# The low-rank product of a four-layer residual chain: x_hi against both halves of the adapters in one matmul, and the gates' part of h2 with the adapters as weights

## Time and profile before

| what | value |
|---|---|
| median of three runs | 701.98 us |
| the profiled execution | 701.46 us |
| its span | 699.6 us |
| granted clock of TensorE, mean | 1.0 |
| busy VectorE, ScalarE, GpSimd | 49%, 40%, 13% |
| phase 2 of group 0 | from 250.23 us |

### The profile page before, as it was taken

One profiled execution on the slowest core, in us unless ns is written; L12 is line 12 of the kernel. 1 busy time (PEld: TensorE's weight loads), 2 busy tenths in 40 slices (PEclk: granted clock), 3 DMA queues, 4 the chain that ended last, 5 costly groups with the idle time before them and its releaser, 6 DMA issues.

```text
span 699.6 us, 9550 instructions
## 1 busy us (share of the span) xinstructions
PE 674.9 (96%) x3432; PEld 581.4 (83%) x3432; DVE 345.9 (49%) x529; ACT 276.7 (40%) x415; POOL 87.6 (13%) x128
## 2 busy tenths in 40 slices
PE   4899999999999999999999999999999999999997
PEld 4789989899999988788789878789878878887886
DVE  4779999999822355025633022741321652302352
ACT  4637484955422442115640022652121553012353
POOL 2300115003010021001210000211000121000020
PEclk9999999999999999999999999999999999999999
DMA  9921312001000115002881001694000586000272
GB/s 258 330 79 30 91 31 61 1 4 57 1 0 1 61 48 217 0 1 95 292 297 60 0 0 40 227 308 167 0 0 0 168 276 230 11 1 0 91 231 100
DMA packets 39315, 67.61 MB, mean 97 GB/s; under 512 B 3572, under 2 KB 23028, under 8 KB 39284
## 3 DMA queue, kind: packets, MB, share of 16 engines
q1 hardware_dynamic: 34672, 58.81, 26.3%
q10 hardware_dynamic: 4612, 8.39, 3.3%
HBM read 58.80 MB, written 8.39 MB: 96 GB/s over the span
## 4 chain that ended last, share of the span: by engine, by line
PE 75%; DVE 10%; ACT 6%; DMA 4%; SPq 2%; issue 2%; POOL 1%; ACTq 0%; DVEq 0%
PE ps L916 25%; PE ps L917 24%; PE ps L918 24%; DVE tmp L737 3%; ACT tmp L502 2%; DMA raw<-w_t 2%; DVE ring_lo L667 2%; DMA e_lo_w<-w_t 2%; DVE w_w L746 1%; DVE tmp L740 1%; DVE w_w L727 1%; DVE w_w L733 1%; DVE tmp L743 1%; ACT raw L480 1%; PE ps L1059 1%
## 5 line engine op out<-in xcount | busy, mean ns | idle before, releaser
L916 PE MATMUL ps<-e_hi,ring_hi 128*128 128x384 f32 (+3 forms) x384 | 134.2, 349 | 11.5 <-DVE e_lo L667 10.1
L667 DVE TENSOR_TENSOR ring_lo<-raw,ring_hi 128x512 fp32r<-128x512 f32 x128 | 89.5, 718 | 91.2 <-ACT ring_hi L594 91.0
L918 PE MATMUL ps<-e_hi,ring_lo 128*128 128x384 f32 (+3 forms) x384 | 133.9, 349 | 0.0
L594 ACT ACTIVATE ring_hi<-raw 128x512 fp32r<-128x512 f32 x128 | 78.2, 628 | 76.7 <-PE ps L918 49.7
L916 PE MATMUL ps<-x_both,e_hi 128*128 128x512 f32 x256 | 102.2, 399 | 2.5 <-DVE e_mid L897 2.5
L916 PE MATMUL ps<-ring_hi,e_mid 128*128 128x512 f32 x256 | 100.0, 391 | 3.6 <-DVE ring_lo L667 3.6
L917 PE MATMUL ps<-x_both,e_hi 128*128 128x512 f32 x256 | 101.2, 395 | 0.0
L918 PE MATMUL ps<-x_both,e_lo 128*128 128x512 f32 x256 | 100.7, 393 | 0.0
L917 PE MATMUL ps<-ring_lo,e_mid 128*128 128x512 f32 x256 | 99.7, 389 | 0.0
L918 PE MATMUL ps<-ring_hi,e_mid 128*128 128x512 f32 x256 | 99.6, 389 | 0.0
L916 PEld LDWEIGHTS ps<-e_hi,ring_hi 128*128 128x128 f32 x384 | 72.7, 189 | 17.3 <-DVE e_lo L667 10.1
(11 more groups left out here) (140 smaller groups left out, 902.6 us busy)
## 6 DMA issues: line engine op xcount, KB each, us to landing
raw<-w_t SPq DMA_DIRECT2D x64, 512.0 KB, 4.8
w_w<-w SPq DMA_DIRECT2D x16, 512.0 KB, 5.0
xraw<-x_t SPq DMA_DIRECT2D x16, 512.0 KB, 4.5
y<-tmp ACTq DMA_DIRECT2D x32, 256.0 KB, 3.2
e_lo_w<-w_t SPq DMA_DIRECT2D x4, 512.0 KB, 10.1
e_lo_w<-w_t SPq DMA_DIRECT2D x4, 384.0 KB, 5.8
e_mid_w<-bs SPq DMA_DIRECT2D x24, 64.0 KB, 2.7
e_mid_w<-b_cat SPq DMA_DIRECT2D x1, 512.0 KB, 7.6
```

The source lines that it names most:

```text
L594: act.activation(ring_hi[:, (2 * k + h) % 4, :], raw[:, k % RAW, h * 512:(h + 1) * 512], ACT.Copy).then_inc(w3_hi, 1)
L667: return dve.tensor_tensor(out, whole, hi.bitcast(F32), ALU.subtract)
L916: pe.matmul(out, a[0], b_[0], start=start, stop=False, **kw)
L918: return pe.matmul(out, a[1], b_[0], start=False, stop=stop, **kw)
```

## The change

Three things change together.

1. `low_rank`. The two halves of E now lie in one tensor, and one matmul with x_hi as weights has both halves moving. The tile is 152 columns (128 + 8 + the 16 of its own sequence only), so this matmul has 2 x 152 = 304 columns, in two runs of SBUF, and the one with x_lo has 152. Each token tile has a bank of its own, 4 to 7, with the two parts side by side. ScalarE copies the right part to SBUF (`tok`) and VectorE adds the left one; only then do the logits start. `low_rank` waits for `y_free` at 8g + 8 instead of 8g + 4.
2. The order in the tile: sequence 0's adapter columns stand behind the logits, sequence 1's ahead of the experts. GpSimd's `now` makes one copy over both halves where it made two; in group 0 the second sequence's columns are in place already.
3. h2. `turn_h2` moves ahead of `turn_g`, takes the adapter columns out of `tok` and writes bank 5. `h2_add` then has br_now as weights (32 columns, zero in the other sequence's place) and the gated tiles moving, 256 columns at a time, 6 matmuls, added in bank 5. The factor 2 moves to the copies out of bank 5.

```diff
-EW = EC + 2 * R2
-TW = ER + NE + 2 * R2
+EW = EC + R2
+TW = ER + NE + R2
+SLOT = [7 if i == 1 else 3 + i // 2 if i % 2 else i // 2 for i in range(NB)]
+TILE_AT = [A0, A0 - R2]
...
+        tok = mid_w[:, 8704:8704 + 4 * TW].rearrange("p (t c) -> p t c", t=4)
...
-            pool.memset(h2_tok[:, :, :], 0.0).then_inc(s_ident, 1)
-            pool.wait_ge(s_ident, 3)
+            pool.memset(br_now_hi[:, :, :].bitcast(F32), 0.0).then_inc(s_ident, 1)
+            pool.memset(br_now_lo[:, :, :].bitcast(F32), 0.0).then_inc(s_ident, 1)
+            pool.wait_ge(s_ident, 4)
...
-                    pool.tensor_copy(e_hi[:, :, at_col:at_col + R2], e_hi[:, :, cols]).then_inc(now_ready, 1)
-                    pool.tensor_copy(e_lo[:, :, at_col:at_col + R2], e_lo[:, :, cols]).then_inc(now_ready, 1)
+                        pool.tensor_copy(e_both[:, :, :, to:to + R2], e_both[:, :, :, cols]).then_inc(now_ready, 1)
...
+            pool.wait_ge(q_dve, step_of(PAIRS - 1, ROUNDS - 1, 1))
+            pool.memset(h2_tok[:, :, :], 0.0).then_inc(h2_clear, 1)
...  (ScalarE, group)
                 split_w3(g, 0, 0)
                 split_w3(g, 0, 1)
+                act.wait_ge(t_done, g + 1)
+                act.activation(tok, ps[:, 4:8, TW:2 * TW], ACT.Copy).then_inc(part_done, 1)
+                act.wait_ge(tok_done, g + 1)
+                act.wait_ge(h2_clear, 1)
+                for j in range(2):
+                    act.activation(h2_tok[:, 2 * j:2 * j + 2, R2 * j:R2 * (j + 1)],
+                                   tok[:, 2 * j:2 * j + 2, NOW_AT[j]:NOW_AT[j] + R2], ACT.Copy).then_inc(h2_tok_done, 1)
                 act.wait_ge(gate, GATE_STEPS * g + GATE_DV)
...
-                act.wait_ge(h2_mm, g + 1)
-                for j in range(2):
-                    (h2_tok from ps, scale=2.0)
                 act.wait_ge(h2t_mm, g + 1)
-                act.activation(h2_k[0:32, :], ps[0:32, 7, :], ACT.Copy).then_inc(h2_hi_done, 1)
+                act.activation(h2_k[0:32, :], ps[0:32, 5, :], ACT.Copy, scale=2.0).then_inc(h2_hi_done, 1)
...  (VectorE, gating)
-                dve.wait_ge(t_done, g + 1)
+                dve.wait_ge(part_done, g + 1)
+                dve.tensor_tensor(tok, ps[:, 4:8, 0:TW], tok, ALU.add).then_inc(tok_done, 1)
+                dve.wait_ge(tok_done, g + 1)
...  (TensorE)
             def low_rank(g):
-                pe.wait_ge(now_ready, 8 * (g + 1))
-                pe.wait_ge(y_free, KT * g + 4)
+                pe.wait_ge(now_ready, 6 * (g + 1))
+                pe.wait_ge(y_free, KT * g + 8)
                 for k in range(KT):
                     for t in range(4):
-                        ins = product(ps[:, 5 + j, (t % 2) * TW:(t % 2 + 1) * TW],
-                                      (x_hi[:, k, cols], x_lo[:, k, cols]), rhs, ...)
+                        pe.matmul(ps[:, 4 + t, 0:2 * TW].rearrange("p (h c) -> p h c", h=2), x_hi[:, k, cols],
+                                  e_both[:, :, k, ecols], start=k == 0, stop=False, skip_group_check=True)
+                        ins = pe.matmul(ps[:, 4 + t, 0:TW], x_lo[:, k, cols], e_hi[:, k, ecols],
+                                        start=False, stop=k == KT - 1, skip_group_check=True)
...
             def h2_add(g):
                 pe.wait_ge(gt_done, g + 1)
-                for t in range(4):
-                    ins = product(ps[:, 5 + j, c0:c0 + R2], (gt_hi[:, cols], gt_lo[:, cols]),
-                                  (br_now_hi[:, j, :], br_now_lo[:, j, :]), ...)
-                ins.then_inc(h2_mm, 1)
+                for j in range(2):
+                    cols = slice(2 * j * P, 2 * (j + 1) * P)
+                    ins = product(ps[0:32, 5, cols], (br_now_hi[:, j, :], br_now_lo[:, j, :]),
+                                  (gt_hi[:, cols], gt_lo[:, cols]), False, True, skip_group_check=True)
+                ins.then_inc(h2t_mm, 1)
...  (TensorE, group)
                 low_rank(g)
                 x3_main(g, 1)
                 x3_main(g, 2)
+                turn_h2(g)
                 turn_g(g)
                 x3_main(g, 3)
                 h2_add(g)
                 x3_main(g, 4)
-                turn_h2(g)
```

More of the change, by code:

```diff
@@ L126, in place @@
                 return whole.enter_context(nc.sbuf_tensor(name, shape, F32))
-            e_lo_w = place("e_lo_w", [P, KT, EW])
-            e_mid_w = place("e_mid_w", [P, KT, EC])
+            e_lo_w = place("e_both_w", [P, 2, KT, EW])[:, 1, :, :]
+            mid_w = place("e_mid_w", [P, KT * EC + R2 * 2])
             w0_w = place("w0_w", [P, KT, D])
@@ L144, in build @@
         br_lo = sb("br_lo", [P, A0], F32R)
-        br_now_hi = sb("br_now_hi", [P, 2, R2], F32R)
-        br_now_lo = sb("br_now_lo", [P, 2, R2], F32R)
-        h2_tok = sb("h2_tok", [P, 4, 2 * R2], F32)
+        br_now_hi = sb("br_now_hi", [P, 2, 2 * R2], F32R)
+        br_now_lo = sb("br_now_lo", [P, 2, 2 * R2], F32R)
         ident = sb("ident", [P, P], F32)
@@ L176, in build @@
         h2_k = mid[0:96, 8192:8704]
-        g_tok = mid_w[:, 8704:9216].rearrange("p (t c) -> p t c", t=4)
-        bs_raw = mid_w[0:96, 9216:10240]
+        tok = mid_w[:, 8704:8704 + 4 * TW].rearrange("p (t c) -> p t c", t=4)
+        bs_raw = mid_w[0:96, 8704 + 4 * TW:9728 + 4 * TW]
+        h2_tok = scales[:, :, :, :].rearrange("p a k e -> p (a k e)").rearrange("p (t c) -> p t c", t=4)
         gt_hi, gt_lo = bc_hi[:, 0:TG], bc_lo[:, 0:TG]
@@ L269, in build @@
         gt_done = sem("gt_done")
-        h2_mm = sem("h2_mm")
+        part_done = sem("part_done")
+        tok_done = sem("tok_done")
+        h2_clear = sem("h2_clear")
         h2_tok_done = sem("h2_tok_done")
@@ L437, in _, with now @@
                     add_identity(w0_raw(m)[:, m, :]).then_inc(ring_diag, 1)
-            def now(g):
-                pool.wait_ge(h2_mm, g)
+            def now(g, first):
+                pool.wait_ge(h2t_mm, g)
                 for j in range(2):
-                    cols, at_col = bass.ds(U0 + R2 * j + 2 * R2 * g, R2), EC + R2 * j
-                    pool.tensor_copy(e_hi[:, :, at_col:at_col + R2], e_hi[:, :, cols]).then_inc(now_ready, 1)
-                    pool.tensor_copy(e_lo[:, :, at_col:at_col + R2], e_lo[:, :, cols]).then_inc(now_ready, 1)
-                    pool.tensor_copy(br_now_hi[:, j, :], br_hi[:, cols]).then_inc(now_ready, 1)
-                    pool.tensor_copy(br_now_lo[:, j, :], br_lo[:, cols]).then_inc(now_ready, 1)
+                    if j == 0:
+                        cols, to = bass.ds(U0 + R2 * g, R2), EC
+                    else:
+                        cols, to = slice(A0 - R2, A0) if first else bass.ds(U0 + 3 * R2 + R2 * g, R2), A0 - R2
+                    if j == 1 and first:
+                        pool.sem_inc(now_ready, 1)
+                    else:
+                        pool.tensor_copy(e_both[:, :, :, to:to + R2], e_both[:, :, :, cols]).then_inc(now_ready, 1)
+                    own = slice(R2 * j, R2 * (j + 1))
+                    pool.tensor_copy(br_now_hi[:, j, own], br_hi[:, cols]).then_inc(now_ready, 1)
+                    pool.tensor_copy(br_now_lo[:, j, own], br_lo[:, cols]).then_inc(now_ready, 1)
             def w3_identity(g, j, k):
@@ L875, in gating @@
                     for t in range(2):
+                        part = tok[:, 2 * j + t, A_AT[j]:A_AT[j] + ER].rearrange("p (e r) -> p e r", e=NE)
                         step_ins = dve.tensor_tensor(
-                            g_tok[:, 2 * j + t, :].rearrange("p (e r) -> p e r", e=NE),
-                            ps[:, 5 + j, t * TW:t * TW + ER].rearrange("p (e r) -> p e r", e=NE),
-                            oh[:, 2, 2 * j + t, :].unsqueeze(2).to_broadcast([P, NE, R1]), ALU.mult)
+                            part, part, oh[:, 2, 2 * j + t, :].unsqueeze(2).to_broadcast([P, NE, R1]), ALU.mult)
                         step_ins.then_inc(g_done, 1)
@@ L893, in group @@
                 dve.wait_ge(h2_hi_done, 2 * (g + 1))
-                minus(h2_k[64:96, :], ps[0:32, 7, :], h2_k[0:32, :]).then_inc(h2_done, 1)
+                dve.scalar_tensor_tensor(out=h2_k[64:96, :], in0=ps[0:32, 5, :], scalar=2.0,
+                                         in1=h2_k[0:32, :].bitcast(F32), op0=ALU.mult, op1=ALU.subtract
+                                         ).then_inc(h2_done, 1)
                 for m in range(KT):
@@ L1034, in x3_close, with turn_h2 @@
                 ins.then_inc(x3_mm, 1)
+            def turn_h2(g):
+                pe.wait_ge(h2_tok_done, 2 * (g + 1))
+                for t in range(4):
+                    pe.matmul(ps[0:32, 5, t * P:(t + 1) * P], h2_tok[:, t, :], ident[:, :],
+                              start=t == 0, stop=False, skip_group_check=True)
             def turn_g(g):
                 pe.wait_ge(g_done, 4 * (g + 1))
-                pe.wait_ge(y_free, KT * g + 8)
                 for t in range(4):
-                    ins = pe.transpose(ps[:, 7, t * P:(t + 1) * P], g_tok[:, t, :], ident[:, :])
```

(2 more changed lines are left out.)

51 lines of the change are left out of this document (16 added, 35 removed).

## The result

The changed kernel takes 694.61 us at the median of four runs (693.11 to 697.30), the one before 701.99 (700.78 to 702.25). The ratio is 0.9892, 95% interval 0.9868 to 0.9916: faster by 1.1%. The forecast was 690.4 with a range from 687.6 to 694.6; the median lies at the range's upper end. The profiled execution took 693.11 (span 691.3), 8.35 less than the one before, where 11.1 was forecast.

A forecast was written before the change was run, and what follows sets the result against it. PE bounds the kernel: phase 2 is a queue of matmuls, each costing the larger of its columns and a weight load. Gains of 1.1 + 3 x 3.33 = 11.1 us off 701.46 give 690.4, range 687.6 to 694.6.

The forecast's parts named there:

- The low-rank product: In low_rank, 32 units of two matmuls at 0.251 us replace three-matmul units: 10.72 to 8.03 per group, saving 2.69.
- One load under one matmul: On PE, only one weight load hides under a matmul; a pitch is the larger of its columns and 0.1117 us.
- rival A: In low_rank, loads run further ahead where wide and narrow matmuls alternate: a unit costs 0.223, total 687.7 us; 8%.
- B: In low_rank, the wide matmul is dearer than its columns through its two runs: total 693.9 to 699.0 us; 14%.
- D: In low_rank, a moving operand jumping between two distant places streams at half pace, wide matmul 0.279: total 706.1 us; 4%.
- h2_add: In h2_add, 12 load-bound matmuls (1.34 us) become 6 of 256 columns (0.70): 0.64 saved per group.
- Group 0: In group 0, PE waits about 2.2 us ahead of turn_g, so this group gains 1.1 us where others gain 3.33.
- so I count no clock loss: Behind group 0's wait ahead of turn_g, matmuls keep their pitch, as behind the 2.38 us stall at 27.65: nothing lost.
- the other edits, at nothing: The y_free wait, bank 4, GpSimd's copies, memsets, ScalarE's new waits and the h2 copies were all priced at zero.
- the y products' waits: PE's waits of 1.1 to 1.5 us in the y products of three groups stay unchanged.
- The gates in groups 1 to 3: Between t_done and turn_g, the gates' 7.6 us hide under 12.35 of PE work, with 4.7 to spare.
- its cover in group 0: Ahead of low_rank in group 0, the last y_free credit comes some 0.6 us early, so PE does not wait.

The follow-up runs named there:

- e4: The changed kernel with low_rank's wide matmul taken apart again into two of 152 columns: 700.88 us, ratio 0.9968 to the kernel before.
- e8: The changed kernel run again, unchanged, for a second profile: 694.26 us, ratio 0.9891 to the kernel before.
- e1: The changed kernel with 128 bytes left free behind the tensor mid: 692.32 us, ratio 0.9858 to the kernel before.
- e2: The kernel before with 128 bytes left free behind e_mid: 703.91 us, ratio 1.0022 to the kernel before.
- e5: The changed kernel with 128 bytes free behind mid and turn_g and h2_add one x3 stage later: 688.49 us, ratio 0.9811 to the kernel before.
- e3: The changed kernel with turn_g and h2_add one x3 stage later in all groups: 691.06 us, ratio 0.9833 to the kernel before.

## Why the prediction was right, and where its sum was off

**The low-rank product: right.** Unit 0.251, stage 8.05 us against 8.03, and e4 gives 2.5 to 3.0 per group for it. One load under one matmul also holds where wide and narrow alternate, so rival A fell. The Trainium skill's rule that the prediction quoted beside it ("TensorE: Matmul & The Clock Gate", "Back-to-back issue gap"), 131 ns for each matmul of 512 columns, does not hold for this kernel's fp32r stream: its matmuls of 512 columns take 227 to 233 ns each. The two runs of the moving operand cost nothing that shows, 0.142 for 0.139: B and D fell.

**h2_add: right**, 0.70.

**Group 0: the wait was foreseen, its whole price was not.** 1.89 was measured for 2.2 forecast; `g_done` stayed tied to the first weight tiles, and the addition took 0.79 for 0.80. The step that failed is "so I count no clock loss". It rested on one stall of the same length in phase 1 behind which the clock had held. The clock fell in four of five profiles here, for 1.5 us where it was measured. Where it held (e8), group 0 took 45.75 against 46.99 before, 1.24 gained for the 1.1 forecast.

**What was missing from the sum** is a term for the tensors' places. The part "the other edits, at nothing" named waits and queues, and never asked what the new layout of SBUF does to matmuls that stay as they were. It cost 4.3 us in the pitch of the y products. Net it is less, since slower y products wait less for their tiles: phase 2 differs by 2.7 us between e1 and the changed kernel, by 3.1 between e2 and the kernel before, and by 2.5 between e5 and e3. In the five profiles with the fast pitch the y products' waits add up to 3.6 to 4.2 us, in the seven with the slow one to 2.4 to 2.9.

**Phase 2 in one line.** The forecast took 11.1 from 449.4, 438.3. Measured 442.9. With the pitch of before (4.3 less) and without the low clock (1.5 less) it is 437.1, 1.2 below the forecast. The shorter wait in group 0 makes 0.3, and the y products' waits are 1.2 us less in all (0.71, 0.86 and 0.84 for 1.08, 1.05 and 1.49), where the forecast had them unchanged; 0.3 us the other way is not accounted for. e8, where the clock held in phase 2, measured 441.5, and less 4.3 for its pitch 437.2.

**Luck.** The range held at its very end: 7.4 us were gained at the median where 11.1 were forecast. The range's upper part had been drawn for rival B, a dearer wide matmul; what filled it was the pitch of the y products and the clock, of which no rival spoke. In phase 1, the profiled execution after began phase 2 at 248.40 where the one before did at 250.23. 1.8 of the 8.35 us between the two profiles come from that and are no work of the change: repeated profiles of unchanged kernels had it at 250.54 (before) and 252.88 (changed).

The gates in groups 1 to 3 stayed hidden, and no wait appeared ahead of `low_rank` (its cover in group 0 is 0.8 us by rows 10 and the start at 255.81, where the prediction says 0.6).

## What to carry to other kernels

Price a matmul by the larger of its own columns and the next weight load; fewer and wider matmuls pay exactly when they were bound by loads. Where one engine's chain is tied to something fixed, such as a load's landing, a shorter stage above it turns into idle time, and idle time of a couple of microseconds can cost nearly as much again through the clock (here 1.5 behind 1.89): put one more block of matmuls in between. When an edit changes the size of a tensor, compare the pitch of a matmul that it doesn't touch in both traces before believing any sum, and expect part of what it costs to come back where a wait for something fixed follows.

## What the runs showed that was not expected

- A 512-column fp32r matmul of the y products takes 0.2269 us where weights and moving operand lie a multiple of 256 bytes apart in SBUF, and 0.232 where they do not (12 profiles, no exception). x3_main's pitch is 0.232 to 0.233 in every kernel; in e1 its first feature tile also has weights and x a multiple of 256 apart and is no faster. So the distance is not the whole rule, and the rest of it is open; so is why the distance counts at all.
- The granted clock fell to 1.2 GHz behind 1.89 us of idle in one execution and not behind 2.04 us in another of the same kernel. The cost of a wait of this length is a chance here, not a fixed sum; what decides it is open.
- e4's twelve runs lie within 700.45 to 701.83, those of the kernel before beside them within 700.61 to 705.22. The clock explains part of such a spread: the seven of those 23 executions of the kernel before that took more than 703.5 us had mean clocks of 0.995 to 0.998. There is no trace of them, so where in them it fell isn't shown, and why e4 is free of it is open.
